# In-place decay scan, a second XH buffer, a fifth exponentials buffer, and newly written orders for all five engines

## The reference, cut to what matters

```
# layer 0: 16-head cross attention
q, k, v = relu(x@Wq+bq), relu(c@Wk+bk), relu(c@Wv+bv)       # heads of 16
a = softmax(where(mask, q k^T / 4, 1e-9))
x = layernorm(a v + x) * gamma + beta
# layer 1: mamba2 block, then 8-head cross attention
zxbcdt = rms(x) @ in_proj                                   # 256 -> 1288
xBC = silu(conv4(xBC));  dt = softplus(dt + dt_bias);  decay = exp(dt*A)
h_t = h_{t-1}*decay_t + (dt_t x_t) B_t^T;  y_t = h_t C_t    # 8 heads of 64, 128 states
h = x + rms((y + D_skip*x) * silu(z)) @ out_proj
out = h + softmax(ln(h)@Wq1 (c@Wk1)^T / sqrt(32) + pad) (c@Wv1) @ Wo
```

## Time and profile before

| what | us |
|---|---|
| runs of the kernel | 1339.41, 1339.72, 1336.35; median 1339.41 |
| span of the profiled execution | 1337.2 |
| PE busy | 1291.6 (97%) |
| DVE busy | 1208.1 (90%) |
| ACT busy | 1130.8 (85%) |
| POOL busy | 928.7 (69%) |

### The profile page before, as it was taken

One profiled execution on the slowest core, in us unless ns is written; L12 is line 12 of the kernel. 1 busy time (PEld: TensorE's weight loads), 2 busy tenths in 40 slices (PEclk: granted clock), 3 DMA queues, 4 the chain that ended last, 5 costly groups with the idle time before them and its releaser, 6 DMA issues.

```text
span 1337.2 us, 43414 instructions
## 1 busy us (share of the span) xinstructions
PE 1291.6 (97%) x15624; PEld 1148.0 (86%) x15624; DVE 1208.1 (90%) x3056; ACT 1130.8 (85%) x3407; POOL 928.7 (69%) x1200
## 2 busy tenths in 40 slices
PE   5879999999999999999999999999999999999987
PEld 4668889988888998889998889989888898888875
DVE  6789999999999999999999999999999989999982
ACT  5658989888889988888988888998888898888875
POOL 3366777777767777777777776777777777766774
PEclk9889999999999999999999999999999999999999
DMA  6102221212221112222121222211222221111110
GB/s 203 40 34 72 69 77 38 70 56 69 77 77 62 52 49 69 77 77 77 38 66 60 69 77 77 61 53 50 69 77 77 71 71 34 62 56 57 49 57 25
DMA packets 41283, 87.00 MB, mean 65 GB/s; under 512 B 5744, under 2 KB 10992, under 8 KB 41072
## 3 DMA queue, kind: packets, MB, share of 16 engines
q1 hardware_dynamic: 40208, 83.81, 19.7%
q10 hardware_dynamic: 864, 0.42, 0.1%
HBM read 75.53 MB, written 8.68 MB: 63 GB/s over the span
## 4 chain that ended last, share of the span: by engine, by line
PE 87%; DVE 4%; ACT 4%; issue 2%; DMA 1%; POOL 1%; SPq 1%; ACTq 0%; DVEq 0%
PE bank L319 26%; PE bank L422 10%; PE bank L550 6%; PE bank L412 5%; PE bank L379 5%; PE bank L533 5%; PE bank L436 4%; PE bank L564 4%; PE bank L669 4%; PE bank L360 3%; PE bank L604 3%; PE bank L625 2%; PE bank L654 2%; PE bank L470 2%; PE bank L416 1%
## 5 line engine op out<-in xcount | busy, mean ns | idle before, releaser
L951 DVE SCALAR_TENSOR_TENSOR ACC<-bank,cw,ACC 128x250 f32<-128x250 f32 (+2 forms) x576 | 264.1, 462 | 5.9 <-ACT ACC L1535 3.3
L319 PE MATMUL bank<-xnT,wnl 128*128 128x256 f32 x640 | 201.6, 315 | 3.3 <-DVE xnL L883 2.3
L1622 ACT ACTIVATE PC<-bank,stc 128x128 f32<-128x128 f32 x512 | 182.5, 389 | 7.7 <-DVE stc L1068 4.3
L319 PE MATMUL bank<-xnL,wnh 128*128 128x256 f32 x640 | 180.3, 282 | 0.0
L319 PE MATMUL bank<-xnT,wnh 128*128 128x256 f32 x640 | 179.8, 281 | 0.0
L800 DVE TENSOR_REDUCE sta<-bank 128x4 f32<-128x512 f32 x256 | 163.7, 673 | 7.8 <-PE bank L379 7.5
L977 DVE TENSOR_TENSOR_SCAN L<-DB,id 128x1024 f32<-128x1024 f32 x64 | 146.8, 2293 | 0.8 <-DMA DB<-dec_scratch 0.8
L319 PEld LDWEIGHTS bank<-xnT,wnl 128*128 128x128 f32 x640 | 121.9, 190 | 26.0 <-issue 17.6
L1437 ACT ACTIVATE PTA<-bank 128x512 f32<-128x512 f32 x256 | 133.3, 628 | 9.0 <-PE bank L416 5.3
L1916 POOL TENSOR_TENSOR PC<-PC,stc 128x512 f32<-128x512 f32 x128 | 132.1, 1042 | 11.3 <-DVE stc L1075 11.3
L319 PEld LDWEIGHTS bank<-xnL,wnh 128*128 128x128 f32 x640 | 122.4, 191 | 0.0
(11 more groups left out here) (210 smaller groups left out, 4709.9 us busy)
## 6 DMA issues: line engine op xcount, KB each, us to landing
DB<-dec_scratch SPq DMA_DIRECT2D x64, 512.0 KB, 4.0
cT<-in_cT SPq DMA_DIRECT2D x64, 256.0 KB, 2.6
xT<-in_xT SPq DMA_DIRECT2D x32, 256.0 KB, 4.0
xt<-in_xt SPq DMA_DIRECT2D x32, 256.0 KB, 3.8
out_x<-X SPq DMA_DIRECT2D x32, 256.0 KB, 4.0
QM<-qm_rows SPq DMA_DIRECT2D x32, 128.0 KB, 4.1
XC<-in_win SPq DMA_DIRECT2D x2, 644.0 KB, 6.7
PTC<-in_wout SPq DMA_DIRECT2D x2, 256.0 KB, 6.6
```

The lines of the kernel that those rows point to most:

```text
L319: mm = e.matmul(t[:, c0:c0 + T], wt[:, k, m:m + 128], x[:, k, :], start=(n == 0), stop=(n == 5))
L951: e.scalar_tensor_tensor(out=w, in0=t[:, 0:T].rearrange("p (b t) -> p b t", b=NB)[:, :, 0:125 + k], scalar=cw[:, c, k:k + 1], in1=w, op0=A ...
L1622: op = e.activation(PC[n % 4][:, p, :], t[:, p * 128:(p + 1) * 128], ACT.Exp, bias=stc[g % 4][:, 4 * i + p:4 * i + p + 1], accum_out=stc[g ...
```

## The change

- The tile `L` is gone. `scan(g,b)` writes over `DB[b]`, `lg` works there in place and `y` reads it there. `scan` no longer waits for a `y`. `dec_in(g,b)` waits until `y` two sequences earlier has run (before: until the scan two sequences earlier had).
- `XH` has two buffers, one for each `b`; `xhe` waits for the `y` two sequences earlier.
- `PTA` has five buffers instead of four; `eA` number n waits for `av` number n-5 instead of n-4.
- All five engines have new orders (prologue, loop, epilogue), and `USES` has new banks. The steps and their instructions are the same.

```diff
-        PTA = ring("PTA", 4, [128, 4, 128])
+        PTA = ring("PTA", 5, [128, 4, 128])
...
-        L = sb("L", [128, 8, 128])
-        XH = sb("XH", [128, 512])
+        XH = ring("XH", 2, [128, 512])
...
+        L = lambda b: DB[b][:, :].rearrange("p (h t) -> p h t", h=8)
...
                     if ns >= 2:
-                        e.wait_ge(s_l, ns - 1)
+                        e.wait_ge(s_y, ns - 1)
                     e.dma_start(DB[b][:, :], scratch[g, b * 1024:(b + 1) * 1024].rearrange(
...
-            load_x(0); load_c(0); load_m(0); load_x(1); load_t(0); load_c(1); load_m(1); load_m(2); load_x(2); load_c(2)
-            load_x(3); load_x(4); load_t(1); load_c(3); dec_out(0); dec_in(0, 0); load_m(3); dec_in(0, 1); load_m(4)
...
+            load_t(0); load_x(1); load_m(0); load_m(1); load_c(1); load_x(2); load_x(3); load_c(2); dec_out(0)
+            dec_in(0, 0); dec_in(0, 1); load_t(1); load_m(2); load_c(3); load_x(4); load_u(0); load_c(4); load_m(3)
...
-                                      XH[:, h * 64:h * 64 + 64], L[:, h, :], start=True, stop=True)
+                                      XH[b][:, h * 64:h * 64 + 64], L(b)[:, h, :], start=True, stop=True)
...
-                    if ns > 0:
-                        e.wait_ge(s_y, ns)
                     if ns == 0:
                         masks()
                     e.wait_ge(d_db[b], 16 * (g + 1))
-                    e.tensor_tensor_scan(L[:, :, :].rearrange("p h t -> p (h t)"), DB[b][:, :],
+                    e.tensor_tensor_scan(DB[b][:, :], DB[b][:, :],
                                          id8[:, :, :].rearrange("p h t -> p (h t)"), 0.0, ALU.mult, ALU.add).then_inc(s_l, 1)
...
-                    if n >= 4:
-                        e.wait_ge(s_av, n - 3)
+                    if n >= 5:
+                        e.wait_ge(s_av, n - 4)
...
-                    if ns > 0:
-                        e.wait_ge(s_y, ns)
+                    if ns > 1:
+                        e.wait_ge(s_y, ns - 1)
                     e.wait_ge(s_bx, ns + 1)
-                    e.activation(XH[:, :], t[:, :], ACT.Copy).then_inc(s_xh, 1)
+                    e.activation(XH[b][:, :], t[:, :], ACT.Copy).then_inc(s_xh, 1)
```

More of the change, by code:

```diff
@@ L296, in sync @@
+            dec_in(0, 0); dec_in(0, 1); load_t(1); load_m(2); load_c(3); load_x(4); load_u(0); load_c(4); load_m(3)
+            load_m(4); load_t(2); dec_out(1); dec_in(1, 0); dec_in(1, 1); load_u(1); load_m(5); load_t(3); load_x(5)
+            dec_out(2); dec_in(2, 0); dec_in(2, 1); load_c(5); load_x(6); load_u(2); dec_out(3); load_t(4)
+            load_m(6); load_c(6)
+            for g in range(NG - 8):
                 dec_in(g + 3, 0)
-                load_m(g + 6)
                 load_x(g + 7)
+                load_m(g + 7)
@@ L299, in sync @@
                 load_u(g + 3)
                 dec_in(g + 3, 1)
+                store(g)
+                dec_out(g + 4)
                 load_t(g + 5)
[L302 to L305 removed]
@@ L306, in sync @@
[L306 to L310 removed]
+                load_c(g + 7)
@@ new lines, in sync @@
+            dec_in(NG - 5, 0); store(NG - 8); load_m(NG - 1); dec_in(NG - 5, 1); load_u(NG - 5); load_x(NG - 1)
+            dec_out(NG - 4); load_c(NG - 1); dec_in(NG - 4, 0); dec_in(NG - 4, 1); load_t(NG - 3); load_t(NG - 2)
+            load_u(NG - 4); dec_out(NG - 3); dec_in(NG - 3, 0); dec_in(NG - 3, 1); store(NG - 7); load_u(NG - 3)
+            dec_out(NG - 2); store(NG - 6); dec_in(NG - 2, 0); dec_in(NG - 2, 1); load_u(NG - 2); load_t(NG - 1)
+            dec_out(NG - 1); dec_in(NG - 1, 0); load_u(NG - 1); dec_in(NG - 1, 1); store(NG - 5); store(NG - 4)
@@ L1672, in scalar @@
[L1672 to L1676 removed]
+            split_x(0); split_c(0); qe(0, 0); ke(0, 0); split_x(1); split_c(1); ke(0, 1); qe(0, 1); ve(0, 0)
@@ new lines, in scalar @@
+            th(4, 3); nt_(5, 1); ac(4, 5); ke(6, 1); oa(5, 0); th(4, 4); eA(5, 4); th(4, 5); eA(5, 5); eA(5, 6)
+            eA(5, 7)
+            for g in range(2, NG - 6):
+                split_x(g + 5)
+                split_c(g + 5)
+                oa(g + 3, 1)
+                zt(g + 2, 1)
+                pC(g, 0)
+                xhe(g + 2, 0)
+                hx(g + 1, 0)
+                hx(g + 1, 1)
+                pC(g, 1)
+                xhe(g + 2, 1)
+                he(g + 1, 0)
+                pC(g, 2)
+                qe(g + 5, 0)
+                ke(g + 5, 0)
+                he(g + 1, 1)
+                qe(g + 5, 1)
+                n1(g + 3, 0)
+                n1(g + 3, 1)
+                q1e(g + 1, 0)
+                pC(g, 3)
+                nx(g + 3, 0)
+                nx(g + 3, 1)
+                q1e(g + 1, 1)
+                ve(g + 5, 0)
+                nh(g + 3, 0)
+                nh(g + 3, 1)
+                qq(g + 2, 0)
+                yh(g + 2, 0)
+                oT(g, 0)
+                eC(g + 1, 0)
+                eC(g + 1, 1)
+                de(g + 3, 0)
+                de(g + 3, 1)
+                ac(g + 3, 0)
+                de(g + 3, 2)
+                eC(g + 1, 2)
+                dq(g + 3, 0)
+                zt(g + 3, 0)
+                ac(g + 3, 1)
+                th(g + 3, 0)
+                qq(g + 2, 1)
+                eC(g + 1, 3)
+                nt_(g + 4, 0)
+                v1e(g + 1, 0)
+                ac(g + 3, 2)
+                dd(g + 3, 0)
+                yh(g + 2, 1)
+                th(g + 3, 1)
+                split_u(g + 2)
+                da(g + 3, 0)
+                ac(g + 3, 3)
+                eA(g + 4, 0)
+                eA(g + 4, 1)
+                eA(g + 4, 2)
+                ac(g + 3, 4)
+                eA(g + 4, 3)
+                th(g + 3, 2)
+                th(g + 3, 3)
+                nt_(g + 4, 1)
+                ac(g + 3, 5)
+                ke(g + 5, 1)
+                oa(g + 4, 0)
+                th(g + 3, 4)
+                eA(g + 4, 4)
@@ new lines, in gpsimd @@
+            for g in range(2, NG - 6):
+                lo_x(g + 5)
+                lo_c(g + 5)
+                xd(g + 2, 0)
+                xr(g + 3, 1)
+                rs(g + 3, 0)
+                rs(g + 3, 1)
+                nC(g, 3)
+                qm(g + 5, 0)
+                nr(g + 3, 0)
+                nr(g + 3, 1)
+                xd(g + 2, 1)
+                ga(g + 2, 0)
+                s2_(g + 2, 0)
+                dx(g + 2, 1)
+                yl(g + 2, 0)
+                ga(g + 2, 1)
+                r2(g + 2, 0)
+                nC(g + 1, 0)
+                qm(g + 5, 1)
+                s2_(g + 2, 1)
+                yl(g + 2, 1)
+                lo_u(g + 2)
+                hr(g + 2, 0)
+                r2(g + 2, 1)
+                dx(g + 3, 0)
+                nC(g + 1, 1)
+                hr(g + 2, 1)
+                nC(g + 1, 2)
+                xr(g + 4, 0)
```

921 lines of the change are left out of this document (392 added, 529 removed), and 22 rows, old and new, of the table USES.

## The result

The changed kernel takes 1420.36 us (median of 4 runs, 1419.36 to 1421.4) against 1338.53 before; ratio 1.0617, 95% interval 1.06 to 1.0634. I had forecast 1335.0. The profiled execution has a span of 1419.4 us, 82.2 more than before.

A forecast was written before the change was run, and what follows sets the result against it. TensorE's own steps were taken to bound the middle. Middle −3.9, fill 0, drain −0.5 gave −4.4 on the 1337.2 us span: 1332.8, plus 2.2 for the median, 1335.0 us; range 1326 to 1344.

The forecast's parts named there:

- The sum in the middle: TensorE in the loop: fewer exits from tiled work, more narrow ends; net −0.14 us a group, −3.9 us over 32 groups.
- Rival 2: Second `y` of a group waits for `lg` on VectorE: 0.5 us for each of 26 bodies, 1348 us; chance 0.10.
- the one on tiles: Trainium skill's rule that changing the tiling mode drains TensorE, so entries and shape changes cost too; the forecast's prices count exits alone.
- The fill: Prologue: later weights, layernorm behind `masks()`, fewer TensorE exits; taken as 0, from −4 to +6 us.
- the late weights: Prologue loads moved behind `load_x(3)`, by up to 8 us; could make the fifth `eA` between nothing and 4 us late.
- The drain: End of the kernel, serial per group: same steps, second `XH` readies `xd` sooner; −0.5 us, from −2 to +2.
- The buffers: In-place scan in `DB`, two `XH`, five `PTA`: remove waits that cost nothing where TensorE is full; priced at 0.
- The exits: TensorE leaving tiled work for a full-array step: 0.15 to 0.19 us each; 229 become 171, 9.9 us gained.
- rival 4: Every tile-shape change on TensorE costs 0.15, −0.45 us a group: 1327.5 us; chance 0.14, shared with other gains over 8 us.

The follow-up runs named there:

- The experiment in the old order: Old orders with the new buffers (1335.11 us), the loop's first scan of a group moved five steps down VectorE's order: 1369.64 us.
- the stats in place of the scan: Changed kernel, each group's first scan cut to 128 of 1024 columns, six bn_stats ahead of it: 1385.9 us; same edit in the old order: 1344.4 us.
- the small `lo_x` and `lo_c`: Changed kernel with GpSimd's lo_x and lo_c made over 16 of 256 columns each: 1381.56 us, period 40.0.

## Why the prediction was wrong

**The step that failed** is the one in "The sum in the middle", and the sentence it rests on: that in the middle the time is the sum of TensorE's own steps, where faster work or a shorter wait elsewhere can gain nothing. The sum then took it that the new orders elsewhere could cost nothing either. The earlier trace rows show TensorE full for the old orders only. I carried it over to new orders on five engines and looked at one meeting point only, `y(g,1)` and `lg`. The runs showed in its place a chain of 41.2 us through four engines: 2.3 us less work for GpSimd, which the sum left out, gave back 1.2 us a group. The term "middle", −3.9, measured +40.0 over 22 periods and 27 more in the first seven groups. What holds the period at 40.0 once GpSimd is relieved, 0.5 us above the old orders, stays open.

**Rival 2** had the right kind and sign and the wrong place and size. TensorE does wait at a `y`, but at the first, and for the bank that the first row maximum of `sA` frees: both halves of `sA` and `y` now stand together, so `y` follows that maximum at once. Ahead of that maximum in VectorE's order stand `x2` and `bs`, and they wait for GpSimd's two `xr`. I gave it 0.5 us a group and a chance of 0.10. The period grew by 1.74, of which TensorE's wait at that `y` shows 0.4; the rest of the same loop shows ahead of other steps. My range ended at 1344, before even my own value of 1348 for it.

**The durations.** I summed VectorE's way to `lg` from mean durations of the trace of before. In the new order VectorE's instructions had 2.6 us a group more duration (`xs` 1.1, `x2` 0.55, `nw` 0.5 and others), and GpSimd's `xr` 1.5. The experiment in the old order shows that `xr` is long where the scan stands beside it, and the stats in place of the scan show that this is worth 1.04 of the 1.74 us in the new order. The Trainium skill states the mechanism, in its page "SBUF — State Buffer", section "SBUF: two separate sides": VectorE and GpSimd have one pair of ports in common, and whichever starts first, a GpSimd instruction or a VectorE instruction in a two-port mode, holds it for its whole length while the other blocks. A VectorE instruction with two SBUF inputs does so too, but only against a GpSimd instruction that reads SBUF. The traces agree, in `xr` (0.73 to 2.6 us beside the scan) and `xs` (0.48 to 1.57 beside `lo_c`), all with two inputs in SBUF, and `bn_stats` with one input stayed at 0.41 to 0.42. It was the rule to weigh, ahead of the one on tiles.

**The fill** I took as 0, from −4 to +6. It was +8.5 to `y(0,0)`. What I had priced, the late weights, went from 21.29 to 27.79 in SP's queue and held nobody up. What I had not priced was `q`, `k` of group 1 ahead of the first `sA`, which came 4 to 6 us later in every run with the new orders. Putting ScalarE's and GpSimd's steps for group 0 first did not bring it back. The clock may have a part in the rest: among kernels with this start, `y(0,0)` came at 88.5 where the granted clock from 40 to 60 us was 0.66, and at 83.2 in one kernel and 87.0 in another where it was 0.83, as it was before the change. How much of the 8.5 is order and how much clock stays open. Of the 27 us from `y(0,0)` to `y(7,0)`, the small `lo_x` and `lo_c` gave back 9. 7.5 us of TensorE's waits there are, as in the middle, waits of `y` for the first row maximum; the others are waits of 0.3 to 2.5 us on `sT`, `y`, `o` in changing places. I did not trace them to one cause, and that stays open.

**The drain**: −0.5 was +6.6. From `y(29,0)` to the end it took 115 to 118 us in every run with the new orders and 110 to 111 with the old. No experiment looked for the cause.

**What held.** The buffers: 0 predicted, −0.1% measured, with an interval that ends at no change. The exits: one more cost at most 0.22, predicted 0.17, though the time of that run was a miss. TensorE's own work of 39.4 to 39.45 against 39.5 has the sign of −0.14, but no run reached a period that shows it. The −0.45 a group of rival 4 did not show.

## What to carry to other kernels

Where one engine is busy all the time, the others' slack is not their idle share: it is the slack of the longest chain that the written orders close over one loop body, and a new order makes new chains. Before predicting a reordering, walk one period of the new order from a step back to itself through every engine, above all over the bank or buffer that each TensorE step waits for. A duration in a trace holds only beside the neighbours it had there: for steps of VectorE and GpSimd ask which of them overlap, and look for one and the same line with a longer mean.

## What the hardware showed that I had not expected

Where a VectorE and a GpSimd instruction exclude each other, the wait is counted as busy time of the one that waits and has no releaser in the list of waits. With the same 3056 instructions VectorE's busy time rose by 58.5 us and GpSimd's by 49, and each engine's share fell or stayed, so neither looked slower. `tensor_reduce` from PSUM (675 ns against 672) and `bn_stats` from SBUF (0.42 us against 0.41) were not touched; the scan (2.46 us against 2.28), `scalar_tensor_tensor` (`xs`, 1.57 against 0.48) and `tensor_tensor` (`nw`, 0.67 against 0.17) with both inputs in SBUF were.
